# Softmax sums moved from SBUF to SBUF, and the router's products on four column strips

## The chip, the cores and the metric

The kernel runs on one core of a Trainium2 chip. The metric is the device time of one execution in microseconds (us), the median of several runs; lower is better.

## What is computed

Four batches of 1024 tokens with 256 channels go through cross attention to 77 context rows (16 heads of 16 channels, some context rows masked), then through a mixture of eight experts with a fixed capacity of 640 rows each. Cut to what matters:

```
x = x + attention(layernorm(x), ctx, ctx, mask)   # q, k, v = . @ W.T + b
        # scores = q k / sqrt(16), masked -> softmax over 77 -> . v -> @ Wo.T + bo
x = x + moe(layernorm(x))
        # t = rows; probs = softmax(t @ Wr)   (Wr: 256 x 8); idx = argmax; pmax = max
        # pos = place of the token among those of its expert; kept = pos < 640
        # out = relu(t @ W1[idx]) @ W2[idx] * pmax if kept, else t
```

All of it is float32, apart from small helpers.

## The kernel before

The 4096 tokens are cut into 8 groups of 512 (`NG = 8`, `GT = 512`), each of 4 token tiles of 128 (`TPG = 4`). The function `pipeline` calls a step function on each engine, with five groups in flight: `a` (first layer norm and transposes), `n` (query, and the maxima of the scores by `natural_scores` on TensorE and `row_maxima` on VectorE, 8 pieces of each per group), `c` (scores, exponentials and weighted values, in four rounds), `r` (softmax division, output projection, residual, second layer norm) and `o` (router, choice of expert, places, scatter of the rows to DRAM). The order of the work on each engine is the order in which its step function is written: TensorE, VectorE, ScalarE, GpSimd and the DMA queue of SyncE (called SP) each go through their own list, and wait on semaphores. After the eight groups come the eight experts, one after the other, from row tiles that are read back.

Around the change:

- `weigh_values` makes, for round `r` of group `c`, a PSUM bank of four strips of 32 partitions. Each strip is one head: 16 rows of weighted values (`DH = 16`) and then rows that all hold the sum of the exponentials. ScalarE copies the bank to `attnU[:, r, :]` (`copy_attn`, line 604).
- SP stores each of the four banks to DRAM (`store_strips`, line 356) and reads the value rows back, packed without gaps, into `attnC` (`pack_strips`, line 363). It waits for the store before the read. After the fourth store it also reads the 16 rows of sums back, as 64 rows of 128, into `sums` (`load_sums`, line 370).
- VectorE inverts the sums (`invert_sums`, line 768, after the first of the eight `row_maxima` of the step). SP stores the inverses to DRAM (line 376), waits until they have landed, and reads them back with each row repeated over the 16 rows of its head into `recip`, by two DMAs (line 381). VectorE multiplies `attnC` by `recip` (`normalise_attn`, line 774) between the third and the fourth `row_maxima`. The projection on TensorE (`project`, line 1105) needs that product.
- In the fifth stage the router's product is `wr_sb` (8 columns per half of the channels) against the transposed rows `tT`, for all 512 tokens at once, into 8 partitions (`router_logits`, line 1130). ScalarE copies the 8 x 512 values (line 626), and TensorE turns them by four transposes (`transpose_logits`, line 1136).
- The weights of the first two experts, 2 MB each, are loaded by SP in the steps `c == 1` and `c == 2`, just ahead of `spread` in the queue.

## Time and profile before

| | |
|---|---|
| median of three runs | 593.15 us (592.21 to 597.88) |
| profiled execution, own time | 595.47 us |
| its span in the profile | 593.7 us |
| TensorE (PE) busy | 487.0 us, 82% of the span |
| VectorE (DVE), ScalarE (ACT), GpSimd (POOL) busy | 199.4, 155.4, 199.9 us |
| mean granted TensorE clock | 0.908 of full speed |

The eight groups of attention and routing take the first 351 us, the experts the rest. Busy shares say which engine has most to do; what sets the end is read from the chain of work that ended last and from the waits. A time in a row is in us from the start of the span unless it says ns.

### The profile page before, as it was taken

Reading aid. Unit: us, or ns where it says so; the run is one execution under the profiler, and the core shown is the slowest. Engines: PE = TensorE matmul, PEld = TensorE weight load, DVE = VectorE, ACT = ScalarE, POOL = GpSimd, SP = SyncE. Lnnn points to the kernel's source line nnn. Section 1 sums busy time; section 2 is a strip of 40 time slices with the busy share of each in tenths; the row PEclk is TensorE's granted clock in tenths of the full one; section 3 lists DMA queues with packets and bytes.
Section 4 is the critical chain, followed back from the end, with each engine's and each line's share of the span. In section 5 each row is a group of like instructions: output and inputs, shape, how many; then the busy total and the mean of one; then the engine's idle time right before and its main releaser. Section 6 shows DMA issues by size and latency. Waiting matters only on the chain.

```text
span 593.7 us, 7701 instructions
## 1 busy us (share of the span) xinstructions
PE 487.0 (82%) x2865; PEld 322.2 (54%) x2865; DVE 199.4 (34%) x576; ACT 155.4 (26%) x224; POOL 199.9 (34%) x312
## 2 busy tenths in 40 slices
PE   3858785969989799997734319999999999999992
PEld 1423232425343343442312118899998999998891
DVE  2143342634556374645324312211212122212110
ACT  0103451542636255554510101101101011111100
POOL 5663260340756648415160640311111111112211
PEclk9967897997989799998967658999999999999997
DMA  7980253251322323242431140603305042416000
GB/s 199 315 241 2 71 162 101 79 183 63 114 97 87 124 75 125 95 134 82 133 97 53 62 149 0 201 28 97 126 19 199 18 155 68 170 51 204 14 28 1
DMA packets 45770, 62.62 MB, mean 105 GB/s; under 512 B 4402, under 2 KB 33625, under 8 KB 45728
## 3 DMA queue, kind: packets, MB, share of 16 engines
q1 hardware_dynamic: 40672, 53.79, 28.6%
q0 software_dynamic: 3456, 7.26, 3.5%
q10 hardware_dynamic: 1600, 1.01, 0.7%
q8 instruction: 27, 0.44, 0.3%
q14 instruction: 15, 0.12, 0.1%
HBM read 36.62 MB, written 27.67 MB: 108 GB/s over the span
## 4 chain that ended last, share of the span: by engine, by line
PE 67%; DMA 15%; DVE 8%; issue 4%; POOL 2%; ACT 1%; SPq 1%; ACTq 0%; POOLq 0%; DVEq 0%
PE tps L1233 10%; PE wk L1243 9%; PE tps L1253 9%; PE wk L1261 9%; PE wk L1105 6%; PE wk L1017 6%; DMA attn_mem<-inverse_sums 6%; PE nat L1040 5%; DMA inverse_sums<-rsum 4%; DMA strips<-shared 3%; PE tps L1060 3%; PE wk L1089 3%; DVE rowmax L745 2%; PE nat L1035 2%; DVE attn_mem L774 2%
## 5 line engine op out<-in xcount | busy, mean ns | idle before, releaser
L562 POOL DMA_INDIRECT out_x<-attn_mem,dest x40 | 39.0, 975 | 198.2 <-DVE attn_mem L943 195.5
L597 ACT ACTIVATE shared<-tps,mask_key 77x1024 f32<-77x1024 f32 x64 | 67.5, 1104 | 29.0 <-PE tps L1064 29.0
L745 DVE TENSOR_REDUCE rowmax<-nat 128x8 f32<-128x616 f32 x64 | 51.1, 798 | 66.2 <-PE nat L1040 65.7
L1233 PE MATMUL tps<-shared,w_sb 128*128 128x256 f32 x256 | 59.3, 392 | 0.6 <-ACT shared L652 0.6
L437 POOL TENSOR_SCALAR ln<-mv 128x4 f32<-128x4 f32 x16 | 3.9, 241 | 162.3 <-DVE mv L797 122.6
L1243 PE MATMUL wk<-w_sb,shared 128*128 128x256 f32 x256 | 57.7, 379 | 0.0
L1253 PEld LDWEIGHTS tps<-shared,w_sb 128*128 128x128 f32 x480 | 56.0, 192 | 0.8
L1253 PE MATMUL tps<-shared,w_sb 128*128 128x128 f32 x480 | 56.0, 275 | 0.0
L1233 PEld LDWEIGHTS tps<-shared,w_sb 128*128 128x128 f32 x256 | 50.5, 198 | 8.3 <-issue 1.0
L1261 PE MATMUL wk<-w_sb,shared 128*128 128x256 f32 x240 | 54.3, 379 | 0.0
L1243 PEld LDWEIGHTS wk<-w_sb,shared 128*128 128x128 f32 x256 | 48.1, 190 | 6.2
L1040 PE MATMUL nat<-kblk,qT 64*128 64x308 f32 x256 | 50.3, 471 | 0.0
L1105 PE MATMUL wk<-wo_sb,attn_mem 128*128 128x256 f32 x128 | 39.7, 464 | 10.6 <-DVE attn_mem L774 9.7
L1261 PEld LDWEIGHTS wk<-w_sb,shared 128*128 128x128 f32 x240 | 44.5, 190 | 5.4
L1035 PE MATMUL nat<-mask_row,tile_heads 64*128 64x308 bf16 x128 | 21.2, 324 | 31.6 <-DVE rowmax L745 30.7
L1035 PEld LDWEIGHTS nat<-mask_row,tile_heads 64*128 64x128 bf16 x128 | 6.9, 94 | 71.8 <-issue 65.6
L943 DVE SCALAR_TENSOR_TENSOR attn_mem<-wk,x_sb 128x256 f32<-128x256 f32 x31 | 15.0, 484 | 81.8 <-PE wk L1261 41.8
L458 POOL TENSOR_SCALAR xn<-x_sb,mv,ln 128x256 f32<-128x256 f32 x32 | 40.8, 1286 | 0.9
L1105 PEld LDWEIGHTS wk<-wo_sb,attn_mem 128*128 128x128 f32 x128 | 27.8, 228 | 22.5 <-DVE attn_mem L774 9.9
L1089 PE MATMUL wk<-shared,v_ones 77*32 77x512 f32 x256 | 34.7, 604 | 6.3 <-ACT shared L597 5.3
L1060 PE MATMUL tps<-qT,kblk 32*77 32x512 f32 x256 | 36.9, 648 | 0.7 <-ACT maxT L592 0.7
L501 POOL DMA_INDIRECT slot_rows<-rows,slot x32 | 32.5, 1014 | 13.8 <-issue 10.4
(123 smaller groups left out, 540.1 us busy)
## 6 DMA issues: line engine op xcount, KB each, us to landing
w_sb<-in_w SPq DMA_DIRECT2D x16, 1024.0 KB, 8.6
strips<-shared SPq DMA_DIRECT2D x32, 256.0 KB, 4.2
slot_rows<-zeros SPq DMA_DIRECT2D x1, 5200.0 KB, 21.9
x_sb<-slot_rows SPq DMA_DIRECT2D x8, 650.0 KB, 4.2
x_sb<-in_x SPq DMA_DIRECT2D x8, 512.0 KB, 9.2
attn_mem<-strips SPq DMA_DIRECT2D x32, 128.0 KB
attn_mem<-inverse_sums SPq DMA_DIRECT2D x16, 256.0 KB
out_x<-base SPq DMA_DIRECT2D x8, 512.0 KB, 4.4
```

Source lines behind the costliest of these rows:

```text
L458: last = pool.tensor_scalar(xn[:, j:j + 1, :], x_sb[:, group(g, j, 1), :], mv1[:, j, 0:1], rstd1[:, j:j + 1], ALU.subtract, ALU.mult)
L597: act.activation(probsT[0:SK, r % 2, 2 * i:2 * i + 2, :], tps[0:SK, 2 * i:2 * i + 2, :], ACT.Exp, bias=mask_key[:, g // GPB:g // GPB + 1]) ...
L745: dve.tensor_reduce(rowmax[:, j, :, m, :], nat_heads, AX.X, ALU.max).then_inc(rowmax_ready, 1)
L1035: pe.matmul(dst, tile_heads[of, :], mask_row[of, b, :].rearrange("p (i n) -> p i n", i=2), start=True, stop=False)
L1040: last = pe.matmul(dst, qT[g % 2][of, m, j * P:(j + 1) * P], kblk[of, b, m, :, :].rearrange("p (i r) k -> p i (r k)", i=2), start=False, s ...
L1060: pe.matmul(tps[0:SK, q, :], kblk[of, b, m, (q % 2) * 2 + par, :], qT[g % 2][of, m, :], start=True, stop=False)
L1089: last = pe.matmul(bank[q * QUARTER:(q + 1) * QUARTER, :], v_ones[:, g // GPB, h, :], probsT[0:SK, r % 2, q, :], start=True, stop=True)
L1105: last = pe.matmul(wk[0][:, j * D:(j + 1) * D], attnC[g % 2][:, m, at:at + P], wo_sb[:, m, :], start=(m == 0), stop=(m == KD - 1))
L1233: last = pe.matmul(tps[:, quarter, f * two:(f + 1) * two], w1_sb[n % 2][:, k, at * P:(at + 1) * P], tT_slots[n % 2][:, k, 0:two], start=(k ...
L1243: last = pe.matmul(wk[(SC * n + c) % 2][:, 0:D], hidden[:, f, c * P:(c + 1) * P], w2_sb[n % 2][:, f, :], start=(f == 0), stop=(f == FC - 1))
L1253: last = pe.matmul(tps[:, half, f * P:(f + 1) * P], w1_sb[n % 2][:, k, at * P:(at + 1) * P], tT_slots[n % 2][:, k, c * P:(c + 1) * P], sta ...
L1261: last = pe.matmul(wk[(SC * n + c) % 2][:, 0:D], hidden[:, f, 0:P], w2_sb[n % 2][:, f, :], start=(f == 0), stop=(f == FC - 1))
```

## The change

The sums no longer go through DRAM. After each copy of a bank, `gather_sums` takes its four sum rows (partitions 16, 48, 80, 112) straight from `attnU` to 16 rows of `sums`, ahead of the store of the bank. `spread` takes the inverses straight from `rsum` to `recip`, by eight DMAs of 64 KB: one for each half of the channels and each token tile. The copies of the next group's banks wait until the sums before have been inverted (`rsum_ready`), since the gathers read the banks. The inversion waits until the spreads of the group before have landed. The strips still go through DRAM to be packed.

The router's weights are padded with zeros to 32 columns, which GpSimd writes ahead of the load. Each token tile's product goes to a column strip of its own in TensorE's array and to 32 partitions of the bank, so that a single 128 x 128 copy and a single transpose follow.

```diff
-        wr_sb = sb("wr_sb", [P, KD, E])
+        wr_sb = sb("wr_sb", [P, KD, QUARTER])
-        lgT = sb("lgT", [E, GT])
+        lgT = sb("lgT", [P, P])
+        SPREADS = 16 * KD * TPG
+            sp.wait_ge(router_zeroed, 1)
+            sp.dma_start(wr_sb[:, :, 0:E], wr.rearrange("(k p) e -> p k e", p=P)).then_inc(w_attn_loaded, 16)
...
+            def gather_sums(g, r):
+                wait(sp, attnU_ready, ROUNDS * g + r + 1)
+                if r == 0:
+                    wait(sp, rsum_ready, g)
+                sp.dma_start(sums[16 * r:16 * (r + 1), :], attnU[DH:P:QUARTER, r, :].rearrange("p (t n) -> p t n", t=TPG)
+                             ).then_inc(sums_loaded, 16)
+
             def store_strips(g, r):
-                wait(sp, attnU_ready, ROUNDS * g + r + 1)
                 sp.dma_start(strips_dram[g % 2, r], attnU[:, r, :]).then_inc(strip_stored[r], 16)
...
-            def load_sums(g):
-                wait(sp, rsum_ready, g)
-                for r in range(ROUNDS):
-                    wait(sp, strip_stored[r], 16 * (g + 1))
-                sp.dma_start(sums[:, :], strips_dram[g % 2].rearrange("r (q x) n -> r q x n", q=4)[:, :, DH, :]
-                             ).then_inc(sums_loaded, 16)
-
             def spread(g):
 
                 wait(sp, rsum_ready, g + 1)
-                sp.dma_start(rsum_dram, rsum[:, :]).then_inc(rsum_stored, 16)
-                wait(sp, rsum_stored, 16 * (g + 1))
                 wait(sp, attn_ready, KD * g)
-                by_row = rsum_dram.rearrange("(m x t) n -> x m (t n)", m=KD, t=TPG)
                 for m in range(KD):
-                    sp.dma_start(recip[:, m, :], by_row[:, m, :][:, None, :].broadcast_to([HH, DH, GT])).then_inc(recip_spread, 16)
+                    for t in range(TPG):
+                        sp.dma_start(recip[:, m, t * P:(t + 1) * P],
+                                     rsum[m * 32 + t:m * 32 + 32:TPG, None, :].broadcast_to([HH, DH, P])
+                                     ).then_inc(recip_spread, 16)
...
                     for k in range(ROUNDS):
+                        gather_sums(c, k)
                         store_strips(c, k)
-                        if k == ROUNDS - 1:
-                            load_sums(c)
                         pack_strips(c, k)
...
+            pool.memset(wr_sb[:, :, :], 0.0).then_inc(router_zeroed, 1)
...
                 wait(act, strip_stored[r], 16 * g)
+                wait(act, rsum_ready, g)
                 act.copy(attnU[:, r, :], wk[1 if r == 2 else 0][:, :]).then_inc(attnU_ready, 1)
...
-                    act.copy(lgT[:, :], wk[1][0:E, :]).then_inc(lgT_ready, 1)
+                    act.copy(lgT[:, :], wk[1][:, 0:P]).then_inc(lgT_ready, 1)
...
-                wait(dve, sums_loaded, 16 * (g + 1))
-                wait(dve, rsum_stored, 16 * g)
+                wait(dve, sums_loaded, 16 * ROUNDS * (g + 1))
+                wait(dve, recip_spread, SPREADS * g)
                 dve.reciprocal(rsum[:, :], sums[:, :]).then_inc(rsum_ready, 1)
...
-                    last = pe.matmul(wk[1][0:E, :], wr_sb[:, k, :], tT[:, k, :], start=(k == 0), stop=(k == KD - 1))
+                    for j in range(TPG):
+                        last = pe.matmul(wk[1][j * QUARTER:(j + 1) * QUARTER, 0:P], wr_sb[:, k, :], tT[:, k, j * P:(j + 1) * P],
+                                         start=(k == 0), stop=(k == KD - 1))
...
-                for j in range(TPG):
-                    last = pe.transpose(wk[1][:, j * E:(j + 1) * E], lgT[:, j * P:(j + 1) * P], ident[0:E, 0:E])
-                last.then_inc(logits_ps, 1)
+                pe.transpose(wk[1][:, 0:P], lgT[:, :], ident[:, :]).then_inc(logits_ps, 1)
```

On SP's queue, from the fourth round of one group to the first of the next, in a step of the middle, before (`shared` holds `attnU`, `attn_mem` holds `attnC` and `recip`):

```order
L370 DMA sums<-strips 64x1x128 [waits strip_stored2,strip_stored1,strip_stored3,strip_stored0,rsum_ready]
L363 DMA attn_mem<-strips 64x1x512 [waits proj_ps,strip_stored3]
L376 DMA inverse_sums<-rsum 64x128 [waits rsum_ready]
L381 DMA attn_mem<-inverse_sums 128x1x512 [waits attn_ready,rsum_stored]
L381 DMA attn_mem<-inverse_sums 128x1x512
L385 DMA out_x<-base 128x4x256 [waits base_ready]
L356 DMA strips<-shared 128x512 [waits attnU_ready]
L363 DMA attn_mem<-strips 64x1x512 [waits proj_ps,strip_stored0]
```

and now:

```order
L359 DMA sums<-shared 16x1x128 [waits attnU_ready]
L363 DMA strips<-shared 128x512
L370 DMA attn_mem<-strips 64x1x512 [waits proj_ps,strip_stored3]
L379 DMA attn_mem<-rsum 128x1x128 [waits attn_ready,rsum_ready]
L379 DMA attn_mem<-rsum 128x1x128 x7
L385 DMA out_x<-base 128x4x256 [waits base_ready]
L359 DMA sums<-shared 16x1x128 [waits rsum_ready,attnU_ready]
L363 DMA strips<-shared 128x512
L370 DMA attn_mem<-strips 64x1x512 [waits proj_ps,strip_stored0]
```

The gather stands ahead of every store, the two waits for a DRAM store around the inverses are gone, and eight spreads stand where a store and two reads stood.

On TensorE, around the router's product of one group, before:

```order
L1040 MATMUL nat<-kblk,qT 128x2x154 x2
L1130 MATMUL wk<-tT,wr_sb 8x512 [waits tT_ready]
L1130 MATMUL wk<-tT,wr_sb 8x512
L1089 MATMUL wk<-shared,v_ones 32x512 [waits probsT_ready,attnU_ready,tT_ready]
L1089 MATMUL wk<-shared,v_ones 32x512 x3
L1035 MATMUL nat<-mask_row,tile_heads 128x2x154 [waits rowmax_ready,kblk_ready,q_ready]
```

and now:

```order
L1041 MATMUL nat<-kblk,qT 128x2x154 x2
L1133 MATMUL wk<-tT,wr_sb 32x128 [waits tT_ready]
L1133 MATMUL wk<-tT,wr_sb 32x128 x7
L1090 MATMUL wk<-shared,v_ones 32x512 [waits probsT_ready,attnU_ready,tT_ready]
L1090 MATMUL wk<-shared,v_ones 32x512 x3
L1036 MATMUL nat<-mask_row,tile_heads 128x2x154 [waits rowmax_ready,kblk_ready,q_ready]
```

Two products of 512 columns have become eight of 128; nothing else on TensorE has changed its place.

## Rows read from the trace of the kernel before

**Rows 1.** The page, chain of work that ended last, share of the span by engine.

```profile
PE 67%; DMA 15%; DVE 8%; issue 4%; POOL 2%; ACT 1%; SPq 1%; ACTq 0%; POOLq 0%; DVEq 0%
```

**Rows 2.** The chain in order of time, step c = 3: start, us, what.

```profile
155.25 0.94 DVE rsum L768
156.21 2.54 DMA inverse_sums<-rsum
...
159.41 4.40 DMA attn_mem<-inverse_sums
...
163.84 1.29 DVE attn_mem L774 x2
...
166.81 3.57 PE wk L1105 x8
```

**Rows 3.** The chain in order of time, steps c = 1, 4 and 5.

```profile
84.41 0.86 DVE rsum L768
...
96.88 1.29 DVE attn_mem L774 x2
...
186.25 0.94 DVE rsum L768
...
196.13 1.55 DVE attn_mem L774 x2
...
219.97 0.95 DVE rsum L768
...
228.20 1.32 DVE attn_mem L774 x2
...
231.20 1.93 PE wk L1105 x8
```

**Rows 4.** Timeline, in brackets the idle time before and its end.

```profile
155.55 0.58 ACT L604 COPY shared<-wk 128x512 f32<-128x512 f32 x1 [1.02 <-PE wk L1089]
...
165.99 0.31 PE L1035 MATMUL nat<-mask_row,tile_heads 64*128 64x308 bf16 x2 [1.81 <-DVE rowmax L745]
...
230.37 0.31 PE L1035 MATMUL nat<-mask_row,tile_heads 64*128 64x308 bf16 x2 [1.47 <-DVE rowmax L745]
```

**Rows 5.** Windows: length, busy us of each engine, then TensorE clock, DMA share, GB/s.

```profile
167.00:170.00 3.00, 3.00 (x8) 2.13 (x7) 0.65 (x1) 0.00 (x0) 2.92 (x4) 0.50 0.35 104
...
231.00:233.00 2.00, 2.00 (x10) 1.44 (x8) 1.00 (x3) 0.00 (x0) 2.00 (x3) 1.00 0.17 35
```

**Rows 6.** Windows behind the last group's two DMAs to `recip`.

```profile
309.05:310.33 1.28, 0.00 (x0) 0.00 (x0) 0.00 (x0) 0.00 (x0) 0.00 (x0) 0.98 0.00 0
...
313.80:315.00 1.20, 0.00 (x0) 0.00 (x0) 0.00 (x0) 0.00 (x0) 0.00 (x0) 0.50 0.51 183
```

**Rows 7.** Line 381, issue time of its DMAs on SP's queue in ns.

```profile
L381 SPq DMA_DIRECT2D attn_mem<-inverse_sums x16: 577/595/613, 91.3 to 309.7; - x16
```

**Rows 8.** DMA queues (packets, MB, share of 16 engines) and one issue (us to landing).

```profile
q1 hardware_dynamic: 40672, 53.79, 28.6%
...
q10 hardware_dynamic: 1600, 1.01, 0.7%
...
sums<-strips SPq DMA_DIRECT2D x8, 32.0 KB, 2.1
```

**Rows 9.** The chain in order of time, from the last group's strips to its router.

```profile
299.17 4.78 DMA strips<-shared
304.03 2.18 DMA sums<-strips
...
309.70 5.33 DMA attn_mem<-inverse_sums
...
332.99 2.47 PE wk L1130 x4
```

**Rows 10.** Timeline, TensorE: the router's product and the weighted values behind it.

```profile
159.26 1.88 PE L1130 MATMUL wk<-tT,wr_sb 128*8 128x512 f32 x4
...
160.86 1.14 PE L1089 MATMUL wk<-shared,v_ones 77*32 77x512 f32 x8
```

More of the change, by code:

```diff
@@ L95, in xattn_moe @@
         strips_dram = nc.dram_tensor("strips", (2, ROUNDS, P, GT), F32, kind="Internal").ap()
-        rsum_dram = nc.dram_tensor("inverse_sums", (HALF, P), F32, kind="Internal").ap()
         ident = sb("ident", [P, P])
@@ L214, in xattn_moe @@
         sums_loaded = sem("sums_loaded")
-        rsum_stored = sem("rsum_stored")
         recip_spread = sem("recip_spread")
@@ L227, in xattn_moe @@
         consts_cut = sem("consts_cut")
+        router_zeroed = sem("router_zeroed")
         picks_ready = sem("picks_ready")
@@ L341, in _ @@
             sp.dma_start(bo_sb[:, :], bo.rearrange("(a n) -> a n", a=1).broadcast_to([P, D])).then_inc(w_attn_loaded, 16)
-            sp.dma_start(wr_sb[:, :, :], wr.rearrange("(k p) e -> p k e", p=P)).then_inc(w_attn_loaded, 16)
+            sp.wait_ge(router_zeroed, 1)
+            sp.dma_start(wr_sb[:, :, 0:E], wr.rearrange("(k p) e -> p k e", p=P)).then_inc(w_attn_loaded, 16)
             for g in range(2, NG):
@@ L765, in invert_sums @@
             def invert_sums(g):
-                wait(dve, sums_loaded, 16 * (g + 1))
-                wait(dve, rsum_stored, 16 * g)
+                wait(dve, sums_loaded, 16 * ROUNDS * (g + 1))
+                wait(dve, recip_spread, SPREADS * g)
                 dve.reciprocal(rsum[:, :], sums[:, :]).then_inc(rsum_ready, 1)
             def normalise_attn(g):
-                wait(dve, recip_spread, 16 * KD * (g + 1))
+                wait(dve, recip_spread, SPREADS * (g + 1))
                 wait(dve, packed[g % 2], 16 * ROUNDS * (g // 2 + 1))
@@ L809, in choose @@
             def choose(g):
-                logits = wk[1][:, 0:TPG * E].rearrange("p (t c) -> p t c", t=TPG)
+                logits = wk[1][:, 0:P].rearrange("p (t c) -> p t c", t=TPG)[:, :, 0:E]
                 wait(dve, logits_ps, g + 1)
```

## The prediction

> **What bounds the kernel now.** I first read the chain of waits, not the busy shares. TensorE makes up two thirds of it, but DMA has 15% [rows 1], and in order of time that DMA is nearly all in one place, which comes back in every group. In the step of c = 3 [rows 2] the reader sees: the inversion ends at 156.2 us; the inverses go to DRAM (2.54 us to landing), SP issues the read, it lands 4.40 us after the issue of the second of its DMAs, and VectorE multiplies at 163.84. I call the time from the end of the inversion to the start of the multiplication D; here it is 163.84 - 156.19 = 7.65 us. Step c = 2 looks like c = 1 and c = 6 like c = 5, so from [rows 3] D is 96.88 - 85.27 = 11.6 us twice (the DRAM store is queued behind 2 MB of expert weights), 196.13 - 187.19 = 8.9 us once and 228.20 - 220.92 = 7.3 us twice. The last group pays it with nothing beside it [rows 9]: store of the fourth strip 4.78, sums 2.18, then the inverses, the second read landing 5.33 after its issue, at 315.03; D is 7.9. The seventh multiplication is not on the chain.
>
> During D TensorE works through its list and then waits for the `row_maxima` behind the multiplication: 1.81 us at c = 3, 1.47 at c = 5 [rows 4]. That wait has a second price. After the 1.81 us the granted clock stood at 0.50 (the 1.2 GHz level) from 167 to 170 us, and the projection took 3.57 us; after the 1.47 us it stayed at 1.00 [rows 2, 5]. So a step with the fall pays about 1.65 us more (eight passes of the projection at half the rate cost 3.57 us, against 1.93 at c = 5 [rows 2, 3]).
>
> **The new spread.** It replaces store, wait and two reads by eight issues. Line 381's DMAs have the same form and take 0.595 us to issue [rows 7], with the gap 0.61. The last issue starts 7 x 0.61 = 4.3 us after the inversion; a small DMA lands 2.1 us after its issue [rows 8]. So by issue alone D' = 6.4 us. The other limit is the data: 256 packets of 2 KB become 1024 of 512 B. The first byte came 1.28 us after the issue or later, and while only the last read ran, DMA share was 0.51, eight engines of sixteen [rows 6]; source and destination are cut the same way now (eight rows, repeated sixteen times), so I keep eight, with 128 packets each. A packet's price, an estimate from [rows 8]: queue q1 spent 0.286 x 16 x 593.7 / 40672 = 66.8 ns on a mean of 1322 B, q10 0.007 x 16 x 593.7 / 1600 = 42 ns on 631 B; the line through both gives 37 ns at 512 B, and 93 ns at 2 KB, which fits the 183 GB/s of [rows 6] (89 ns). 128 x 37 = 4.7 us, plus 1.3 and some 0.3 to finish: 6.3 us. Both limits meet, so I take 6.5 us with the queue free and 6.8 to 7.3 where GpSimd's scatters run beside it. The bounds are 6.4 us (the issues) and 128 x 66.8 ns + 1.6 = 10.2 us (every small packet at q1's mean).
>
> The Trainium skill is more hopeful on packets ("DMA: Bandwidth & Descriptors", section "Why small descriptors are slow (HBM only)"): a fixed cost of about 3 cycles a packet, and no such penalty from SBUF to SBUF. By its figures a 512 B packet would be an estimated 19 cycles at 850 MHz, 22 ns; D' would sit at the issue limit, the steps with weights would gain some 2 us more each, and the total would be nearer 583 us. No row shows an SBUF to SBUF packet, so the sum goes by the line above.
>
> **What the steps gain.** c = 3: 7.65 - 6.8 = 0.85. c = 4: 8.9 - 7.3 = 1.6. c = 5 and 6: 7.3 - 6.7 = 0.6 each. c = 1 and 2: the weights are still ahead in the same queue until about 91.0 us, then 4.7 us of packets and 0.3 to finish make 96.0 against 96.88; I take 0.6 each for want of anything finer. Together 4.85 us. All of it reaches the chain, since TensorE waits there in each of these steps.
>
> **The last group.** SP's round trip of store, wait and pack sets this stretch. The gather goes ahead of each store, but the store is held by the pack before it anyway (4.78 us here against some 2 with a free queue), so the 0.56 us of a gather's issue costs little, up to 0.3 us a round. The fourth gather no longer waits for the store: sums would be there near 303.5 instead of 306.21 [rows 9]. But SP still waits for the fourth store (now some 304.3) and issues the last pack before it comes to the spread at 304.9; 4.3 + 2.1 from there is 311.3, and with the spread's packets behind the pack's 313.2. Against 315.03 a gain of 1.8 us; bounds 0 and 3.7.
>
> **The router.** Four passes of 512 columns take 1.88 us, 0.47 each [rows 10]. Behind them the weighted values go over four strips of 32 columns: eight passes of 512 columns in 1.14 us, where one after the other they would need 3.8. So strips do run side by side. The new product is 16 passes of 128 columns, 0.118 us each: 4 x 0.118 = 0.5 us if the strips overlap fully, 1.9 if not at all; I take 0.7, since the passes are short against what it costs to start them, and a saving of 1.2 us a group. In the steps it lies inside D: TensorE only comes to its wait 1.2 us sooner. It counts once, for the last group, at the low clock: 2.47 us [rows 9] becomes 1.0, and the copy of 128 instead of 512 columns and three transposes less give some 0.3. Gain 1.8 us.
>
> **The price of waiting longer.** In the steps c = 5 and 6 TensorE would now wait 1.47 - 0.6 + 1.2 = 2.1 us, more than the 1.81 after which the clock fell. I expect it to fall in both: 2 x 1.65 = 3.3 us lost. In the other four steps it falls already.
>
> **Edits priced at nothing.** The copy of a bank now waits for the inversion: the first starts at 155.55 and would wait until 156.2 [rows 2, 4]. Behind it on ScalarE stand the two copies of `tT` and the exponentials, and TensorE's second half of the transposes waits for it; some 0.1 us, inside D. Without that cover it would be 0.65 a step. The gathers need 4 x 0.56 us of SP's issue where one load needed 0.56; in the middle steps SP has a wait of its own ahead of the fourth round that takes this in. GpSimd's fill with zeros and SP's wait for it fall in the first microseconds, behind loads; if that cover failed it would cost once, under 1 us. The load of the sums was not what the inversion waited for in the steps (it stands behind `row_maxima` 0), so its going gains nothing there.
>
> **The sum.** 4.85 + 1.8 + 1.8 - 3.3 = 5.15 us. The profiled execution took 595.47 us for a span of 593.7, so 590.3 like for like; the median is 2.3 us lower, and taking the same difference off it gives 593.15 - 5.15 = **588.0 us**. A change within 1% (5.9 us) is about what a measurement of this kernel can't tell from none.
>
> **Rivals.**
> First, the clock doesn't fall in the two late steps: the waits of 1.47 us were close, and where TensorE's work lies before them shifts too. Then 588.0 - 3.3 = 584.7. Against it: the one step with 1.81 us did fall.
>
> Second, the strips don't shorten the router's product. Then TensorE waits less than before (1.81 - 0.85 = 1.0 us at c = 3, 0.9 at c = 5 and 6), the clock stays up in all three, and the kernel is faster by more: 4.85 + 1.8 + 0.3 + 1.65 = 8.6, 584.6 us. For it speaks only that the passes are four times shorter than those of [rows 10]. The Trainium skill ("TensorE: Matmul & The Clock Gate", section "The mechanism") has a rule that would bring this: a weight load overlaps running products only where the row group differs, and here all strips share the rows. [rows 10] is against it, its strips share their rows too.
>
> Third, **slower**: the small packets. If one costs 55 ns and not 37, the spread's data take 7.0 us and D' is about 8.7 to 9.1 with the usual traffic. Then c = 3 loses 1.1, c = 5 and 6 lose 1.4 each, c = 1 and 2 1.7 each, c = 4 0.1, and the end gains 0 instead of 1.8: -7.4 + 1.8 - 3.3 = -8.9, so 602. It decides from 128 x 7 x (p - 37 ns) = 5.15 us on, p = 43 ns; q10's mean is 42 at 631 B, so this is not far off. For it: DMAs issued in a row on a full queue may also be held up at issue.
>
> Fourth, packets at 25 ns or less: D' at the issue limit everywhere, the weights' steps gaining 2 us each: 583 us.
>
> **Chances.** Forecast 0.44, with a range of its own of 585 to 591; clock stays 0.17; router no shorter 0.07; small packets 0.22; cheap packets 0.10. The range over the cases is 581 to 600: it holds the fast cases and the nearer part of the slow one, whose 602 lies just outside. Since the forecast sits close to the 1% line, I count 0.13 of its 0.44 as faster, 0.30 as same and 0.01 as slower; of the small packets 0.17 as slower and 0.05 as same; of the cheap ones 0.08 as faster. Faster 0.13 + 0.17 + 0.07 + 0.08 = 0.45, same 0.30 + 0.05 + 0.02 = 0.37, slower 0.18.
>
> **What would show it.** Right: eight DMAs from `rsum` issued in about 4.9 us; D' of 6.4 to 7.3 in the middle steps; the router's product near 0.7 us; TensorE's waits at c = 5 and 6 near 2 us with clock 0.50 behind them; the last multiplication near 313. Wrong: an issue on SP that takes well over 0.6 us, multiplications later than 7.7 us after the inversion, a wait of VectorE for the sums, or a clock that stays at 1.00 in the steps c = 5 and 6.

## The result, and the profile after

| | before | after |
|---|---|---|
| median, us | 592.68 | 575.59 |
| lowest and highest, us | 590.51, 597.88 | 574.55, 576.45 |
| profiled execution, us (span) | 595.47 (593.7) | 576.45 (574.6) |

The ratio is 0.9678, with a 95% interval of 0.9628 to 0.9728: the kernel is 17 us faster, and the forecast was 5. The range of 581 to 600 does not hold it. (The ratios here and below are as measured, with their intervals; they differ a little from the quotients of the medians.)

The page of after, with the lines that answer to [rows 1, 8] (chain by engine; queue: packets, MB, share of 16 engines; DMA issues):

```profile
PE 67%; DMA 9%; DVE 7%; SPq 6%; issue 5%; POOL 3%; ACT 1%; ACTq 0%; POOLq 0%; DVEq 0%
...
q1 hardware_dynamic: 46560, 53.53, 29.3%
...
attn_mem<-rsum SPq DMA_DIRECT2D x64, 64.0 KB
```

DMA's share of the chain went from 15% to 9%, and SP's issuing (SPq) now has 6%: the round trip has become a row of issues. The step of c = 3 in order of time, against [rows 2]; first the timeline, then the chain:

```profile
147.87 0.93 DVE L769 RECIPROCAL rsum<-sums 64x128 f32<-64x128 f32 x1
148.83 5.19 SPq L379 DMA_DIRECT2D attn_mem<-rsum  x8
```

```profile
153.42 2.15 DMA attn_mem<-rsum
...
155.59 1.29 DVE attn_mem L775 x2
```

D' = 155.59 - 148.80 = 6.79 us, against 7.65: eight issues 0.65 us apart, and the last one lands 2.15 us after it was issued. It is 6.77 at c = 4 and 6.75 at c = 5. TensorE in the same step, against [rows 4, 10], and two windows of the clock, against [rows 5]:

```profile
152.14 0.65 PE L1133 MATMUL wk<-tT,wr_sb 128*32 128x128 f32 x16
...
153.74 1.06 PE L1090 MATMUL wk<-shared,v_ones 77*32 77x512 f32 x8 [0.95 <-ACT shared L597]
...
157.74 0.31 PE L1036 MATMUL nat<-mask_row,tile_heads 64*128 64x308 bf16 x2 [0.68 <-DVE rowmax L746]
```

```profile
95.00:97.00 2.00, 2.00 (x7) 1.18 (x4) 0.80 (x1) 0.00 (x0) 0.00 (x0) 0.50 0.50 180
...
158.50:160.50 2.00, 2.00 (x12) 1.51 (x12) 0.91 (x2) 0.56 (x2) 2.00 (x3) 1.00 0.12 4
```

The router's product takes 0.65 us instead of 1.88, and TensorE comes so early to the next weighted values that it waits 0.95 us for ScalarE's exponentials; before the change there was no wait at this place of the step. (Elsewhere it waited for exponentials before and after alike.) What is left at the row maxima is 0.68 us, not 1.81, and behind it the clock stays at 1.00. The projection takes 1.99 us in each of the steps c = 3 to 6. At c = 1, in a longer wait, the clock falls:

```profile
94.18 0.44 PE L1036 MATMUL nat<-mask_row,tile_heads 64*128 64x308 bf16 x2 [4.49 <-DVE rowmax L746]
...
95.58 3.78 PE L1106 MATMUL wk<-wo_sb,attn_mem 128*128 128x256 f32 x8
```

That step and its spread, in the chain:

```profile
82.13 0.86 DVE rsum L769
...
87.78 4.22 DMA attn_mem<-rsum
...
92.03 1.29 DVE attn_mem L775 x2
```

D' is 9.04 us (11.6 before), at c = 2 it is 9.27 (11.95). The end of the last group, against [rows 9]:

```profile
285.02 4.11 DMA strips<-shared
...
289.15 0.54 SPq L370
...
294.37 2.45 DMA attn_mem<-rsum
...
296.85 1.30 DVE attn_mem L775 x2
...
314.64 1.60 PE wk L1133 x16
```

Laying the starts of the inversions side by side tells where the 19.1 us between the two spans are (us, before minus after):

| stretch | before | after | difference |
|---|---|---|---|
| start to inversion at c = 1 | 84.41 | 82.13 | 2.3 |
| c = 1 to 2 | 34.51 | 33.32 | 1.2 |
| c = 2 to 3 | 36.33 | 32.42 | 3.9 |
| c = 3 to 4 | 31.00 | 28.49 | 2.5 |
| c = 4 to 5 | 33.72 | 28.50 | 5.2 |
| c = 5 to 6 | 29.02 | 28.47 | 0.5 |
| c = 6 to 7 | 27.80 | 29.18 | -1.4 |
| c = 7 to the last inversion | 29.44 | 26.15 | 3.3 |
| its D | 8.82 | 8.19 | 0.6 |
| last multiplication to the first expert's product | 40.94 | 40.02 | 0.9 |

(The last D is counted here from the start of the inversion.) The first row is not the change: the second query projection took 3.78 us at the low clock in the profiled run of before and 1.98 in that of after, and in the profiles of the fifteen experiments it was 1.98 ten times and 3.78 five times, with and without parts of the change; the inversion of c = 1 started at 83.4 to 84.6 us where it was 3.78, and at 80.2 to 82.4 where it was 1.98. Without the first row 16.8 us are left, close to the 17.1 us between the medians.

### The profile page after: what moved, and what is told of

Same layout as the page of the kernel before. It is cut to its first block, busy times and chain, and to the rows that moved or that the text cites. A ratio compares the mean times of both kernels' runs of the same rounds, so it can differ in the third digit from the quotient of the medians.

```text
span 574.6 us, 7901 instructions
## 1 busy us (share of the span) xinstructions
PE 473.4 (82%) x2937; PEld 317.9 (55%) x2937; DVE 203.4 (35%) x576; ACT 152.6 (27%) x224; POOL 200.3 (35%) x313
## 4 chain that ended last, share of the span: by engine, by line
PE 67%; DMA 9%; DVE 7%; SPq 6%; issue 5%; POOL 3%; ACT 1%; ACTq 0%; POOLq 0%; DVEq 0%
PE tps L1235 10%; PE wk L1245 10%; PE tps L1255 9%; PE wk L1263 9%; PE wk L1106 5%; SPq L379 5%; PE wk L1018 5%; PE nat L1041 5%; DMA attn_mem<-rsum 4%; DMA strips<-shared 3%; PE tps L1061 3%; PE wk L1090 3%; DVE rowmax L746 3%; PE nat L1036 2%; DVE attn_mem L775 2%
## 5 line engine op out<-in xcount | busy, mean ns | idle before, releaser
L1106 PE MATMUL wk<-wo_sb,attn_mem 128*128 128x256 f32 x128 | 36.4, 433 | 6.7 <-DVE attn_mem L775 5.8
L458 POOL TENSOR_SCALAR xn<-x_sb,mv,ln 128x256 f32<-128x256 f32 x32 | 38.9, 1224 | 0.9
L1106 PEld LDWEIGHTS wk<-wo_sb,attn_mem 128*128 128x128 f32 x128 | 26.2, 216 | 17.5 <-issue 6.4
```

What stands on the lines that cost most here:

```text
L1106: last = pe.matmul(wk[0][:, j * D:(j + 1) * D], attnC[g % 2][:, m, at:at + P], wo_sb[:, m, :], start=(m == 0), stop=(m == KD - 1))
```

## The experiments

The kernels of a series ran on the same chip beside the kernel before. Ratios are to the kernel before in the same series; its median was 593.41 in the first (experiments 1 to 4), 592.88 in the second (5, 7, 9, 10), 595.77 in the third (6, 8, 11, 12) and 594.56 in the last, with three kernels (13 to 15).

**1. The router alone.** Before, with the sixteen short passes, the padded weights and the one transpose of the logits:

```diff
-                    last = pe.matmul(wk[1][0:E, :], wr_sb[:, k, :], tT[:, k, :], ...)
+                    for j in range(TPG):
+                        last = pe.matmul(wk[1][j * QUARTER:(j + 1) * QUARTER, 0:P], wr_sb[:, k, :], tT[:, k, j * P:(j + 1) * P], ...)
```

> Only the router's part of the change: padded weights, eight products of 128 columns on four strips, one copy, one transpose; the sums and inverses go through DRAM as before. Theory A (the time from inversion to multiplication, D, sets each step): inside a step the router is hidden, D stays at 7.3 to 12 us, and only the last group gains, about 1 us: 591.5 us; the wait ahead of the fifth row maxima grows, or splits into one for the exponentials and one of about 2 us, and the clock falls behind it as before. Theory B (the router's shorter product is what keeps the clock up, whatever D is): no fall behind the waits of c = 3 and 4, some 4 us: 587 to 588 us.

Measured: 590.76 us, ratio 1.0003 (0.9955 to 1.005). Timeline of TensorE at c = 3 and c = 4:

```profile
163.66 0.31 PE L1038 MATMUL nat<-mask_row,tile_heads 64*128 64x308 bf16 x2 [2.09 <-DVE rowmax L748]
...
164.42 3.67 PE L1108 MATMUL wk<-wo_sb,attn_mem 128*128 128x256 f32 x8
...
194.48 0.31 PE L1038 MATMUL nat<-mask_row,tile_heads 64*128 64x308 bf16 x2 [1.60 <-DVE rowmax L748]
...
195.24 1.99 PE L1108 MATMUL wk<-wo_sb,attn_mem 128*128 128x256 f32 x8
```

The router's part is worth nothing that can be measured, though its product is 1.2 us shorter in each group: in the steps the saving turns into waiting, and not at the row maxima. D at c = 3 is 7.93 us here, 5.84 more than that wait, and in the kernel before it was 7.65 with a wait of 1.81, also 5.84 more; the new wait of 0.95 us for the exponentials is there. The clock fell behind the wait of 2.09 us and not behind that of 1.60.

**2. The sums alone.** After, with the router's part of the diff taken back.

> Only the gather and the spread from SBUF to SBUF; the router as before, 8 columns and 512 rows at once. Theory A: all of the gain but the last group's router, 576.5 us; TensorE comes to its wait 1.2 us later and waits under 0.6 us at c = 3 to 5, clock up. Theory B: without the shorter router the clock falls again in two or three steps, 580 us or more.

Measured: 577.69 us, ratio 0.9722 (0.9654 to 0.979). With the product back at 1.88 us there is no wait of 0.95, and the one at the row maxima is the same as in after:

```profile
151.64 1.88 PE L1129 MATMUL wk<-tT,wr_sb 128*8 128x512 f32 x4
...
157.21 0.31 PE L1033 MATMUL nat<-mask_row,tile_heads 64*128 64x308 bf16 x2 [0.65 <-DVE rowmax L743]
...
157.97 1.99 PE L1103 MATMUL wk<-wo_sb,attn_mem 128*128 128x256 f32 x8
```

So nearly all of the gain is the sums'.

**3. Before, with TensorE busy in the wait.** Products that nobody reads, into a bank that is free there:

```diff
+                if has(c) and has(n):
+                    wait(pe, attnU_ready, ROUNDS * c + 2)
+                    for i in range({1: 12, 2: 12, 3: 3, 4: 3, 5: 3, 6: 3}.get(c, 0)):
+                        pe.matmul(wk[0][:, 0:D], ident[:, :], wq_sb[:, 0, :], start=True, stop=True)
                 if has(n):
                     natural_scores(n, 4)
```

> The kernel before, with products that nobody reads put on TensorE just ahead of its wait in every step: three of 256 columns (about 1.3 us) for c = 3 to 6, twelve (about 5.3 us) for c = 1 and 2. It prices the clock alone, since D and all DMAs stay. If the falls come from TensorE standing still there: clock 1.00 behind all six waits, projections of 1.9 us in place of 3.7, 2.7, 3.6 and 3.7, some 6 us less than before: 586 us. If they depend on the place in time and not on the wait: no change beyond 1 us, 592 us.

Measured: 587.63 us, ratio 0.9872 (0.9799 to 0.9945): work that nobody needs makes the kernel before faster, by 5.8 us in the medians and 7.6 by the ratio. At c = 1 in the timeline of TensorE:

```profile
97.98 0.31 PE L1035 MATMUL nat<-mask_row,tile_heads 64*128 64x308 bf16 x2 [1.03 <-DVE rowmax L745]
98.73 2.00 PE L1105 MATMUL wk<-wo_sb,attn_mem 128*128 128x256 f32 x8
```

The projection is at 1.00 there, at c = 2 and at c = 4 to 6. At c = 3 the multiplication itself came late (D of 9.75), 2.41 us of wait were left, and the projection took 3.68. So the low clock behind these waits is worth some 6 to 8 us of the kernel before, and it is TensorE's idling that brings it.

**4. Eight issues, still by DRAM.** Before, with each of the two reads of the inverses cut into four:

```diff
-                    sp.dma_start(recip[:, m, :], by_row[:, m, :][:, None, :].broadcast_to([HH, DH, GT])).then_inc(recip_spread, 16)
+                    for t in range(TPG):
+                        sp.dma_start(recip[:, m, t * P:(t + 1) * P],
+                                     by_row[:, m, t * P:(t + 1) * P][:, None, :].broadcast_to([HH, DH, P])
+                                     ).then_inc(recip_spread, 16)
```

> The kernel before, with the read of the inverses from DRAM cut into eight DMAs of 64 KB (512 B packets) instead of two of 256 KB. It prices number and size of the DMAs apart from the place they read. If it is the issues that count (0.65 us each), the read takes 4.5 + 2.15 = 6.7 us from the first issue instead of 5.0: D about 9.3 us in the middle steps, 1.6 us more in each of seven groups, some 604 us. If small packets were dear (55 ns) it would be 8.7 us and over 612 us. If neither costs, 593 us.

Measured: 607.6 us, ratio 1.0213 (1.0131 to 1.0295). The chain at c = 3, and what TensorE does behind it:

```profile
157.66 2.61 DMA inverse_sums<-rsum
...
164.67 2.38 DMA attn_mem<-inverse_sums
...
167.07 1.38 DVE attn_mem L777 x2
```

```profile
169.31 0.44 PE L1038 MATMUL nat<-mask_row,tile_heads 64*128 64x308 bf16 x2 [3.68 <-DVE rowmax L748]
170.71 3.78 PE L1108 MATMUL wk<-wo_sb,attn_mem 128*128 128x256 f32 x8
```

D is 9.45 us: the store's 2.6 and then the same eight issues and one landing as in after. With the wait doubled, the clock is low at c = 1 to 4, and in part at c = 5; at c = 6 the projection took 1.99 us behind a wait of 3.25. What the change gains is the round trip by DRAM; cutting the spread into eight costs by itself.

**5 and 6. The two halves of the sums' part.** Experiment 5 gathers the sums from SBUF and leaves the inverses to DRAM; experiment 6 spreads the inverses from SBUF and loads the sums from the strips in DRAM. Both have the old router.

```diff
 # 5, in spread(g)
+                sp.dma_start(rsum_dram, rsum[:, :]).then_inc(rsum_stored, 16)
+                wait(sp, rsum_stored, 16 * (g + 1))
 # 6, in step
-                        gather_sums(c, k)
                         store_strips(c, k)
+                        if k == ROUNDS - 1:
+                            load_sums(c)
```

> One half of the sums part alone: the sums are gathered by four small DMAs from SBUF, but the inverses still go to DRAM and come back by two reads; the router's product as before the change. Theory A (the gain comes from the spread, whose D is shorter by one DRAM round trip): D stays at 7.3 to 11.6 us, only the last group's inversion comes earlier by the store's landing (some 2 us), the steps c = 1 to 6 and their clock stay as before; 590 us, ratio 0.993 to 1.000. Theory B (the store and reload of the sums cost the steps too, by traffic on the queue or SP's waits): TensorE's waits shrink and the clock holds in more steps; 584 us or less, ratio under 0.985.

> The other half of the sums part alone: the inverses are spread by eight DMAs from SBUF, the sums are still loaded from the strips in DRAM, the router's product is as before the change. The gather alone gave 0.9956 and both halves together 0.9722. Theory A (the two act at different places and add, the spread carries nearly all): ratio 0.975 to 0.980, 578 to 581 us, TensorE's waits at c = 3 to 6 near 0.7 us and the clock at 1.00 behind them. Theory B (the spread helps only once the sums come by the short way too): ratio 0.985 or more, with an inversion that waits for its sums in the steps.

Measured: gather 590.78 us, ratio 0.9956 (0.9927 to 0.9985); spread 582.27 us, ratio 0.9758 (0.9688 to 0.9828). Their product is 0.9715, and both together gave 0.9722: within the intervals they add. In experiment 6 TensorE's waits at c = 3 to 6 are 0.70, 0.69, 0.67 and 0.68 us with projections of 1.99; in experiment 5 they are 2.25 and 2.51 at c = 3 and 4 (1.81 and 3.36 in before), and 0.94 and 0.62 at c = 5 and 6. The gather acts on the last group: from the inversion of c = 7 to the last one it is 26.32 us with the gather alone and 28.19 with the spread alone, against 29.44 in before and 26.15 in after. In experiment 5 the last D is 9.96 us (7.88 in before), which eats most of that.

**7. Four wide DMAs.** After, with the inverses in 32 rows of 256 and four spreads of 1 KB packets:

```diff
-                    for t in range(TPG):
-                        sp.dma_start(recip[:, m, t * P:(t + 1) * P],
-                                     rsum[m * 32 + t:m * 32 + 32:TPG, None, :].broadcast_to([HH, DH, P])
+                    for t in range(2):
+                        sp.dma_start(recip[:, m, t * 2 * P:(t + 1) * 2 * P],
+                                     rsum[m * 16 + t:m * 16 + 16:2, None, :].broadcast_to([HH, DH, 2 * P])
```

> The changed kernel with the inverses held as 32 rows of 256 and spread by four DMAs of 1 KB packets, in place of 64 rows of 128 by eight DMAs of 512 B packets. The reciprocal grows from 0.94 to some 1.87 us. Theory A (D is set by SP's eight issues of 0.65 us plus a landing of 2.15): D falls from 6.8 to some 4.3 to 4.8, net 1.1 to 1.5 us less per group; the middle steps can keep only their remaining wait of 0.68, c = 1 and 2 and the end all of it: 571 us. Theory B (D is set by the data, 128 packets a DMA engine or the same bytes): D is 6.0 or more, and with the longer reciprocal nothing is won: 576 to 578 us.

Measured: 583.09 us, ratio 0.9856 (0.9785 to 0.9927), slower than after. The last group in the chain:

```profile
294.18 1.75 DVE rsum L769
...
298.34 5.49 DMA attn_mem<-rsum
...
303.85 1.30 DVE attn_mem L775 x2
```

Theory A is out, and B has the direction but not the size. The last of the four is issued 2.4 us after the first, but it lands 5.49 us after its issue, and D is 303.85 - 295.93 = 7.9 us (also at c = 3), more than with eight. It isn't the count of packets, which is halved. If eight engines carry them, as a DMA share of 0.50 to 0.65 in most of these microseconds suggests, a 1 KB packet costs about (7.9 - 1.6) / 64 = 98 ns, where a 512 B one of after costs at most (6.8 - 1.6) / 128 = 41 (estimates, with the 1.6 us of the prediction for start and end). Experiments 13 and 14 take this up.

**8. A quarter of the bytes.** After, each spread carrying 32 of 128 columns, used four times over:

```diff
-                        sp.dma_start(recip[:, m, t * P:(t + 1) * P],
-                                     rsum[m * 32 + t:m * 32 + 32:TPG, None, :].broadcast_to([HH, DH, P])
+                        sp.dma_start(recip[:, m, t * P:t * P + 32],
+                                     rsum[m * 32 + t:m * 32 + 32:TPG, None, 0:32].broadcast_to([HH, DH, 32])
```

> The changed kernel whose eight spread DMAs carry 32 of the 128 columns each (as many packets, a quarter of the bytes); the multiplication uses those 32 columns four times, so the inverses of the other tokens are left out and the output is not the reference's. Theory A (behind a free queue D is eight issues of 0.65 us plus one landing of 2.15): D stays at 6.7 to 6.8 us at c = 3 to 5, and the time at 573 to 576 us. Theory B (the bytes set D): D falls to 5 us or less at c = 3 to 5; the time falls by TensorE's remaining waits, 0.7 a step, to 571 us or less. At c = 1 and 2, where the weights' traffic lies ahead, A expects D of 9.0 to fall only if bytes and not packets are what drains behind the weights.

Measured: 560.32 us, ratio 0.9419 (0.9347 to 0.9491). The tokens choose other experts here, and the experts' part is 5.5 us shorter, probably for that (from the first expert's product to the end 232.2 us, 237.7 in after), so the total is no measure; up to that product it is 10.8 us ahead of after. The chain at c = 3:

```profile
142.23 0.62 SPq L379
...
146.81 1.78 DMA attn_mem<-rsum
...
148.62 1.29 DVE attn_mem L777 x2
```

D is 6.41 us against 6.79: behind a free queue it is the issues, as theory A had it, and bytes are 0.4 us of the landing. At c = 1 and 2 D falls from 9.04 and 9.27 to 7.15 and 7.03: behind the weights it is the bytes, 2 us of them in each. Those two steps are 6.8 us of the 10.8, the clock that holds behind the shorter wait of c = 2 among it; the rest is 0.4 a step, and a c = 6 without its late landing (D 6.5 us).

**9. Strips packed from SBUF to SBUF.** After, with no strips in DRAM:

```diff
-                sp.dma_start(strips_dram[g % 2, r], attnU[:, r, :]).then_inc(strip_stored[r], 16)
+                for q in range(4):
+                    at = par * HALF + q * DH
+                    sp.dma_start(attnC[g % 2][at:at + DH, m, :], attnU[q * QUARTER:q * QUARTER + DH, r, :]
+                                 ).then_inc(strip_stored[r], 16)
```

> The changed kernel with the strips packed from SBUF to SBUF as well, four DMAs of 16 partitions a round, and no strip in DRAM. Theory A (in the last group SP's chain of store, landing of 2.7 to 4.1 us and pack paces all four rounds): the last inversion comes 6 to 9 us earlier, the middle steps stay near 28.5 us; 568 us. Theory B (VectorE's maxima and TensorE's scores pace the last group just as closely): the strips' waits go to another engine and the time is 573 to 576 us. Rival on the other side: eight more issues of 0.65 us a step put SP behind, the fourth gather comes late and D grows: over 578 us.

Measured: 571.75 us, ratio 0.9632 (0.9584 to 0.968), 3.8 us under after's 575.59 in the medians; the intervals of the two ratios overlap. The last inversion starts at 282.67 instead of 288.66 us, at the edge of theory A's range, but not for its reason. Of these 6.0 us 4.7 are there already at the inversion of c = 7 (257.81 against 262.51). Most come from c = 1 and 2, where D is 7.30 and 7.80 us instead of 9.04 and 9.27 and the stretches to the next inversion are 2.8 and 2.9 us shorter; at c = 6, where the clock fell, 1.3 us are lost again. The last group's round trip by DRAM was worth the rest, 1.3 us: from the inversion of c = 7 to the last one it is 24.86 us, 26.15 in after. The chain has no DMA in that stretch any more; it goes by TensorE, the layer norm's small steps, and `t_sb` on VectorE just ahead of the inversion, as theory B had it:

```profile
281.50 1.04 DVE t_sb L811 x3
...
282.67 0.94 DVE rsum L773
...
288.33 2.07 DMA attn_mem<-rsum
```

The multiplication behind it starts 6.4 us earlier than in after, but the first expert's product only 4.5 (332.39 against 336.87 us). The clock took the difference: the second half of the last projection was slow here and fast in after (timeline of 9, chain of after):

```profile
296.43 3.78 PE L1111 MATMUL wk<-wo_sb,attn_mem 128*128 128x256 f32 x8 [0.88 <-DVE rows L790]
```

```profile
302.69 2.01 PE wk L1106 x8
```

The rows of c = 6 are under experiment 12.

**10. After, with TensorE busy at c = 1 and 2**, six and four unread products as in experiment 3.

> The changed kernel with products on TensorE whose results nobody reads, six at c = 1 and four at c = 2, put into its wait before the fifth row maxima; the only difference is what TensorE does while it waits. Theory A (the wait of 4.5 and 3.2 us lets the clock fall, and the projection behind it then pays): the clock stands at 1.00 behind the remaining wait, the projections of c = 1 and 2 take 1.9 instead of 3.7 and 2.7 us, what comes behind gains some more; 572.8 us. Theory B (the slow projection has another cause): no gain, 575.5 to 577 us.

Measured: 574.65 us, ratio 0.969 (0.9642 to 0.9737), against 0.9678 for after: no gain that can be told. In its timeline the projection at c = 2 is 1.99 us (2.79 in after), at c = 1 it is 3.04 (3.78) behind a wait of 2.48 that was left; 1.5 us together, in the direction of theory A and about half its size.

**11. Weights behind the spread.** After, with the loads of 2 MB at c = 1 and 2 moved:

```diff
-                if c == 1:
-                    load_weights(0)
-                if c == 2:
-                    load_weights(1)
                 if has(r):
                     spread(r)
+                if c == 1:
+                    load_weights(0)
+                if c == 2:
+                    load_weights(1)
```

> The changed kernel with the expert weights of the steps c = 1 and 2 (2 MB each) issued behind the spread instead of ahead of it. Theory A (D of 9.0 and 9.3 us at c = 1 and 2 is the weights' traffic ahead in the queue): D falls to 6.8 in both, TensorE's waits there from 4.5 and 3.2 to some 2.2 and 0.7 us, the clock holds behind the second: 4.7 us less plus 0.7 to 1 for the clock, 570 us. Theory B (the traffic only moves: the strips of the first round behind the weights come late and the inversion of the same step with them): D falls, but the next inversion comes 2 to 4 us later after it, and the time is 574 to 577 us.

Measured: 576.39 us, ratio 0.9641 (0.955 to 0.9731): the same as after. (The profiled execution was the shortest of the four, 570.03 us.) The chain behind the spread of c = 1, and the next inversion in the timeline:

```profile
88.14 8.25 DMA strips<-shared
```

```profile
111.50 0.94 DVE L769 RECIPROCAL rsum<-sums 64x128 f32<-64x128 f32 x1 [1.28 <-DMA sums<-shared]
```

Both theories are half right. D falls to 6.7 and 7.0 us, as A says; the first strips then land 8.25 us after their issue, and the inversion waits for its sums, as B says, by 1.3 us at c = 2 and 0.85 at c = 3.

**12. The parts together.** Experiment 9, the moved weights, and three unread products at c = 1.

> A version that tries to beat both: the changed kernel with the strips packed from SBUF to SBUF (571.75 us by itself), the weights of c = 1 and 2 behind the spread, and three unread products on TensorE in its wait at c = 1. If the parts add: D at c = 1 and 2 from 7.3 and 7.8 to 6.8 (1.5 us), the projection at c = 1 at 1.00 (1.7 us): 568 to 569 us. If the weights' traffic holds up the SBUF to SBUF strips: 571 to 574 us.

Measured: 569.93 us, ratio 0.9572 (0.9509 to 0.9635), the fastest that computes the whole, 5.7 us under after in the medians (the intervals of the two ratios just touch); against experiment 9 the difference is too small to tell. The projections at c = 1 and 2 are 1.99 us, but D is 8.25 and 7.51 us there and not the 6.8 expected. The step c = 6 of experiments 9 and 12 side by side, first 9:

```profile
238.81 0.31 PE L1041 MATMUL nat<-mask_row,tile_heads 64*128 64x308 bf16 x2 [2.25 <-DVE rowmax L750]
239.56 3.67 PE L1111 MATMUL wk<-wo_sb,attn_mem 128*128 128x256 f32 x8
```

```profile
240.77 0.31 PE L1041 MATMUL nat<-mask_row,tile_heads 64*128 64x308 bf16 x2 [2.29 <-DVE rowmax L750]
241.53 1.99 PE L1111 MATMUL wk<-wo_sb,attn_mem 128*128 128x256 f32 x8
```

**13 and 14. Where the source rows lie.** In after each spread reads eight rows four apart, over 32 partitions; in experiment 7 they lay two apart, over 16. Experiment 13 is 7 with rows four apart, experiment 14 is after with eight neighbouring rows:

```diff
 # 13, against 7
-                                     rsum[m * 16 + t:m * 16 + 16:2, None, :].broadcast_to([HH, DH, 2 * P])
+                                     rsum[m * 2 + t:QUARTER:4, None, :].broadcast_to([HH, DH, 2 * P])
 # 14, against after
-                                     rsum[m * 32 + t:m * 32 + 32:TPG, None, :].broadcast_to([HH, DH, P])
+                                     rsum[m * 32 + t * 8:m * 32 + t * 8 + 8, None, :].broadcast_to([HH, DH, P])
```

> The four wide spreads again (32 rows of 256, 1 KB packets), but each DMA now reads eight rows that lie four partitions apart, over partitions 0 to 31, as each of the eight DMAs of the changed kernel does; in the kernel with four wide spreads at 583.09 us they lay two apart, over 16 partitions. The gather takes two DMAs a round for it. Theory A (what made a 1 KB packet cost 98 ns was where the source rows lie): the packets fall to no more than twice the 41 ns of the 512 B ones, D falls from 7.9 to between 5.0 us (2.4 us of issues, a landing of 2.15 and the rest) and 6.8; the time comes back to 572 to 577 us. Theory B (a 1 KB packet, or a DMA of 128 KB, costs that much wherever its rows lie): D stays at 7.5 to 8 us, 581 to 584 us. The Trainium skill (SBUF — State Buffer, section Door 1: The DMA port swizzle) has a rule for A: rows two apart over 16 partitions reach four ports, rows four apart over 32 reach eight.

> The reverse: the changed kernel with its eight spreads of 512 B packets, but each reads eight neighbouring partitions (the inverses of one token tile and half of the heads lie together); the gather takes four DMAs a round, sixteen a group, which puts the last inversion of a group later by up to 1.8 us and is no part of D. Theory A (where the source rows lie): D rises from 6.8 to 8 us or more at c = 3 to 5, the time to 584 us or more. Theory B (it does not matter where they lie): D stays at 6.7 to 6.9, and the time at 576 to 581 us by the later inversions alone.

Measured: 13 took 574.29 us, ratio 0.9678 (0.9584 to 0.9771); 14 took 605.02 us, ratio 1.0199 (1.0078 to 1.032). Timeline of 13 at c = 3, and the chain of 14 there:

```profile
148.42 2.61 SPq L381 DMA_DIRECT2D attn_mem<-rsum  x4
...
153.46 1.29 DVE L777 TENSOR_TENSOR attn_mem<-attn_mem 128x512 f32<-128x512 f32 x2 [0.81 <-DMA attn_mem<-rsum]
```

```profile
152.30 0.95 DVE rsum L771
...
159.88 4.14 DMA attn_mem<-rsum
...
164.05 1.29 DVE attn_mem L777 x2
```

The same bytes, packets and issues: at c = 3 D is 5.1 us with the rows four apart and 7.9 with the rows two apart; 6.8 with the small packets four apart and 10.8 with neighbours (9.7 to 10.9 over the groups). In 14 even SP's issuing is held up, 6.6 us from the first to the last instead of 4.6. Theory A holds, twice, and the rule of the Trainium skill that stands beside it ("SBUF — State Buffer", section "Door 1: The DMA port swizzle") agrees. The 605 us of 14 are not the spread's alone: its twelve more gathers a group were expected to cost up to 1.8 us each group. That 13 is no faster than after in spite of the shorter D has two reasons: 0.8 us of it go to the reciprocal, and in the middle steps only a wait of 0.68 us was left to win. In the medians it is 1.3 us under after, too little to tell.

**15. Wide spreads and direct packing.** Experiments 9 and 13 in one kernel.

> The four wide spreads over 32 partitions and the strips packed from SBUF to SBUF, in search of a version that beats both: beside 571.75 us for the packing alone, if D falls by 1.5 us and the reciprocal costs 0.8 more, 569 to 571 us; if the wide spreads stay slow, 577 us or more.

Measured: 570.06 us, ratio 0.9606 (0.9533 to 0.968), as expected and like experiment 12.

## Why the prediction was wrong

The mechanism of the spread was right and measured close to its numbers; the failed steps are the clock, the steps with weights, and the last group.

**The price of waiting longer (failed).** The forecast had TensorE wait 2.1 us at c = 5 and 6 and the clock fall there, for a loss of 3.3 us, "in the other four steps it falls already". It read a shorter router as a longer wait at the row maxima. In fact a new wait of 0.95 us for ScalarE's exponentials took up the saving of 1.2 us, which the prediction had not looked for: it followed the maxima and not the other inputs of TensorE's list. What was left at the maxima was 0.68 us at c = 3 to 5, and the clock fell at none of the steps c = 3 to 6. (D is 0.86 us shorter, and TensorE comes to this wait 0.26 us later for the copy that waits: 1.12 of the 1.13 us.) So the change did not lose 3.3 us but won the falls that were in before: the projections took 3.57 and 3.71 us at c = 3 and 4 and 1.99 after. At c = 4 the scores ahead of the projection had run at the low clock too, and the fall cost 2.8 us, not 1.65. With the D saved the steps c = 3 and 4 gave 7.7 us where 2.45 were forecast. The first rival (the clock stays in the late steps) was right so far, but it kept the old falls at c = 3 and 4. Experiments 3, 4 and 6 show the size and the sign: fill the waits and the kernel before gains 6 to 8 us, lengthen them and it loses 14 (the longer D among it), shorten them by the spread alone and the clock holds.

**The steps with weights (failed).** Forecast 0.6 each; D fell by 2.6 and 2.7 us. The 4.7 us for the spread's data fit, but their start was wrong: the prediction took the weights to fill the queue until 91.0 us, since the store of the inverses landed then. The traffic itself ends before that. Windows of after and of before:

```profile
87.00:88.00 1.00, 1.00 (x12) 0.34 (x6) 0.00 (x0) 0.25 (x1) 0.00 (x0) 1.00 0.73 219
```

```profile
89.00:90.00 1.00, 1.00 (x10) 0.16 (x11) 0.00 (x0) 0.00 (x0) 0.00 (x0) 1.00 0.84 261
```

In after the DMA share is 0.94 to 1.11 from 82 to 87 us and falls from 1.06 to 0.80 at 87.2, 5.1 us after the inversion's start; 87.2 and 4.7 are 91.9, and the multiplication started at 92.03. In before it is 0.96 to 1.14 from 84 to 89 us and falls from 1.08 to 0.71 at 89.6, 5.2 us after its inversion's start and well ahead of 91.0. That the spread's packets begin where the share falls is inferred; no row shows it. Experiment 8 agrees: with a quarter of the bytes 1.9 to 2.2 us of this goes away. By the Trainium skill ("DMA: Bandwidth & Descriptors", section "Why small descriptors are slow (HBM only)") a packet would be an estimated 22 ns and D at c = 1 at the issue limit; the drain behind the weights is on the side of the 37 ns. These steps gained 1.2 and 3.9 us in all, the first less because the clock fell fully behind its wait of 4.49 us (a projection of 3.78 us, 2.79 in before); at c = 2 it was the other way round.

**The new spread.** Forecast 6.5 to 6.8 us, measured 6.75 to 6.79 at c = 3 to 5. An issue is 0.65 us, not 0.61, and the landing 2.15. Of the two limits it is the issues that hold (experiment 8). At c = 4 the 7.3 was too careful. At c = 6 it was 8.75 (the last landing took 4.13 us) and in experiment 2 some 6.8; what disturbed it is open. The fourth rival (cheap packets, D' at the issue limit everywhere) was right for the middle steps only. The third rival (packets of 55 ns, 602 us) is out here, and experiment 14 shows what it would have taken: with neighbouring source rows D is 10 to 11 us and the time 605, more gathers among it. The line through queues' means that priced a packet had no place for where it comes from.

**The last group.** Forecast 1.8, bounds 0 to 3.7; measured 3.9 (3.3 for the inversion and 0.6 in D). SP was where the prediction saw it: 289.15 pack, 289.78 first spread. But the fourth store landed in 4.11 us and not 4.78, and the earlier ones in 2.69 to 4.08 and not 3.90 to 4.67. Experiments 5 and 6 put the inversion's part down to the gather. It helped less than it could: the fourth gather was issued at 284.42 us, and the inversion waited for its sums until 288.66, 4.2 us and not the 2.1 of a small DMA, with a store right behind it in the queue. Experiment 9, which takes the strips' round trip away, shortens this stretch by only another 1.3 us.

**The router.** The product was forecast at 0.7 us and took 0.65, in the steps; the strips do run side by side. The second rival and the rule behind it (the Trainium skill, "TensorE: Matmul & The Clock Gate", section "The mechanism") are out for these column strips: sixteen passes one behind the other would need 1.9 us. The end was forecast 1.8 us shorter; 2.47 became 1.60 in the chain, and the stretch to the first expert's product is 0.9 us shorter. Experiment 1: nothing in the total.

**Priced at nothing.** The copy that waits for the inversion delayed TensorE's list from the second half of the transposes on by 0.26 us (0.1 forecast), inside D. Of the gathers, the fill with zeros and SP's wait nothing shows.

The sum by the measured terms, without the start: 1.2 + 3.9 + 2.5 + 5.2 + 0.5 - 1.4 + 3.3 + 0.6 + 0.9 = 16.7 us, against 17.1 in the medians. Against the forecast that is 3.9 us more at c = 1 and 2, 5.3 more at c = 3 and 4, 1.2 more at c = 5 and 6, 2.1 more in the last group and 0.9 less for the router.

## What to carry to other kernels

A wait of TensorE has a price beside its length, and a change that shortens one should be counted with the slow work behind it, also in the steps where the clock falls today; a D shorter by 0.9 us was worth 2.5 here, and one shorter by 2.2 was worth 5.2. When an engine's own work gets shorter ahead of a wait, look at every input of its list: the saving can be taken up by another wait (here ScalarE's 0.95 us), so that the known wait gets neither longer nor shorter. For small copies from SBUF, spread the source rows over the partitions before thinking of packet sizes.

## What the runs showed of the hardware

Work that nobody reads, put into TensorE's waits, made the kernel before 1.3% faster (0.9872). The fall behind a wait is not decided by the wait's length alone: behind 2.25 us the projection took 3.67 and behind 2.29 us 1.99, at the same place of nearly the same program; behind 1.81 us it fell in before, behind 2.65 us at c = 6 of after and 3.25 us at c = 6 of experiment 4 it did not. What else decides it is open. What eight source rows feed depends on their places: with each DMA's rows over 8 partitions a spread of 512 KB took 10.8 us (eight DMAs), over 16 it took 7.9 (four), over 32 it took 6.8 (eight) and 5.1 (four). Sixteen passes of 128 columns on four column strips took 0.65 us, 0.04 each.
